# Seven half-size products for z over pairs of tiles

## The chip, the cores and the metric

The kernel runs on one core of a Trainium2 chip. The metric is the device time of one execution in microseconds (us), as the median of several runs. The engines of the core are TensorE (PE, matmuls, with its weight loads as PEld), VectorE (DVE), ScalarE (ACT), GpSimd (POOL) and SyncE (SP), which here only issues DMAs. They run their own queues and wait for each other by semaphores.

## The reference

```python
W = weights[condition]                         # x: (128, 64, 1024); 16 matrices of 64 x 64
y = einsum('bct,bcd->bdt', x, W)
z = einsum('bsd,od->bso', y, W_ffn) + b        # 1024 x 1024
u = einsum('bsd,edr->ebsr', y, A)              # 8 x 16 = 128 low-rank columns
m = einsum('ebsr,ero,e->bso', u, B, p_scores)
gamma = minimum(0.5 * norm(z) / (norm(m) + 1e-6), 1.0)    # norms over the last axis
out = x + z + gamma * m
```

Seen as a matrix, x has 128 x 64 = 8192 rows of 1024; all is float32.

## The kernel before

Two batches of 64 rows make a tile of 128 rows by 1024 columns; there are 64 tiles. The program has a body of four tiles, run once as an opening, in a loop, and once as a closing. All order is written out by hand, one function per engine, and all hand-offs are semaphores with counted waits.

For a tile, PE first mixes (`mix`, L416): for each of 8 chunks of 128 columns, the x chunk is the stationary operand and the block-diagonal 128 x 128 `mixer` of the two batches' matrices the moving one. So y comes out transposed, in two halves of 512 (half h of the 1024 summed columns) in PSUM `mix_ps`. These float32 matmuls appear as two instructions each, 8 a half. ACT casts y to `y_hi` in the fp32r type (L245), and DVE subtracts to get `y_lo` (L333). Every later product is the sum of three passes, hi x hi, hi x lo and lo x hi. W, A and B are held as hi and lo too; they are split once at the start by ACT and DVE (L241, L327).

`down` (L424) computes u for two tiles at once (256 moving columns, 8 chunks x 3 passes), `linear` (L443) half of z's columns for one tile (8 chunks x 3 passes of 512 moving columns, L439), `up` (L449) m for one tile (6 matmuls of 512 columns). DVE adds the bias to z out of PSUM (L368), ACT squares z and m with a row sum (L289, L313), POOL takes the roots as powers of 0.5 (L227, L232) and adds half of the residual x (L224), DVE the other half (L396), forms gamma and adds gamma times m (L408). SP loads x four tiles ahead into four slots, as soon as both residual halves of a tile are done, and stores the result.

PE's order for one tile in the loop: `down` (each second tile), `mix` of the tile two ahead, half 0; `linear` half 0; `up`; `mix` half 1; `linear` half 1. The mixer blocks are copied by ACT out of `cond_all`, which holds all 16 matrices (L248 to L255).

At the start, W arrives in eight chunks of 128 rows by 1024 (L174), tile 0's products follow the chunks, and tile 1's mix stands after the fifth chunk (L478).

Of the kernel before, what the change touches and what calls it, by code (L numbers as in the profile page):

```python
# [5 lines left out]
def conditioned_clamped_low_rank_linear_kernel(  # L6
# [43 lines left out]
    assert (C * PER, XR, H, D % P, TILES % BODY) == (P, P, 512, 0, 0) and STEPS >= 3

    x_tiles = x.rearrange("(n q) c t -> n (q c) t", q=PER)
    out_tiles = out.rearrange("(n q) c t -> n (q c) t", q=PER)

    ctx = ExitStack()
    with ctx:  # L59
# [21 lines left out]
        cond_ids = sb("cond_ids", [1, B], i32)
        p_col = sb("p_col", [P, 1], fp32)
        idle = sb("idle", [P, H], bf16)

        x_in = sb("x_in", [P, BODY, D], fp32)

        y_hi = sb("y_hi", [P, 2, KC, 2 * P], fp32r)
        y_lo = sb("y_lo", [P, 2, KC, 2 * P], fp32r)
# [9 lines left out]
        z_sum = sb("z_sum", [P, 2], fp32)
        half = sb("half", [P, 1], fp32)
        m_sq = sb("m_sq", [P, 2], fp32)  # L100
        norm_z = sb("norm_z", [P, 2], fp32)
        norm_m = sb("norm_m", [P, 2], fp32)
        twice_m = sb("twice_m", [P, 2], fp32)
        half_over_m = sb("half_over_m", [P, 2], fp32)
        gamma = sb("gamma", [P, 2], fp32)

        z_b = rows[:, 0:2, :]
        result = rows[:, 2:4, :]
        w_in = [rows[:, k, :] if k < 4 else w_late[:, k - 4, :] for k in range(KC)]
# [58 lines left out]
        def _(sp):

            sp.dma_start(cond_ids[:, :], condition.rearrange("(o n) -> o n", o=1)).then_inc(ids_loaded, 16)  # L170
            for q in range(PER):
                sp.dma_start(cond_all[q * C:(q + 1) * C, :, :], cond_w).then_inc(cond_loaded, 16)  # L172
            sp.dma_start(x_in[:, 0, :], x_tiles[0]).then_inc(x_loaded[0], 16)
            for k in range(KC):  # L174
                sp.dma_start(w_in[k], w[k * P:(k + 1) * P, :]).then_inc(w_loaded[k], 16)
                if k == MIX_1_AFTER:
                    sp.dma_start(x_in[:, 1, :], x_tiles[1]).then_inc(x_loaded[1], 16)
            sp.dma_start(x_in[:, 2, :], x_tiles[2]).then_inc(x_loaded[2], 16)
            sp.dma_start(a_in[:, :, :], a.rearrange("(k p) e r -> p k (e r)", p=P)).then_inc(a_loaded, 16)
            sp.dma_start(p_col[:, :], p_scores.rearrange("(e o) -> e o", o=1).unsqueeze(1)  # L180
                         .to_broadcast([X, R, 1])).then_inc(p_loaded, 16)
            sp.dma_start(bm_in[:, :], bm.rearrange("e r o -> (e r) o")).then_inc(bm_loaded, 16)
            sp.dma_start(bias[:, :], b.rearrange("(o n) -> o n", o=1).to_broadcast([P, D])).then_inc(bias_loaded, 16)
            for t in range(3, BODY):
                sp.dma_start(x_in[:, t, :], x_tiles[t]).then_inc(x_loaded[t], 16)

            def step(i, first, last):
                for j in range(BODY):
                    t = i * BODY + j
                    if not last:  # L190

                        sp.wait_ge(residual_0_ready, t + 1)
                        sp.wait_ge(residual_1_ready, t + 1)
                        sp.dma_start(x_in[:, j, :], x_tiles[t + BODY]).then_inc(x_loaded[j], 16)
                    if not (last and j == BODY - 1):
                        sp.wait_ge(out_ready, t + 1)
                        sp.dma_start(out_tiles[t], result[:, j % 2, :]).then_inc(out_stored[j % 2], 16)
                    else:

                        for h in range(2):  # L200
                            sp.wait_ge(out_ready, t + h + 1)
                            sp.dma_start(out_tiles[t][:, h * H:(h + 1) * H],
                                         result[:, j % 2, h * H:(h + 1) * H]).then_inc(out_stored[j % 2], 16)

            steps(sp, step)
            sp.wait_ge(out_stored[0], 16 * (TILES // 2))
            sp.wait_ge(out_stored[1], 16 * (TILES // 2 + 1))

        @block.gpsimd
        def _(pool):  # L210
            nc.gpsimd.memset(idle[:, :], 0.0).then_inc(idle_set, 1)
            nc.gpsimd.memset(half[:, :], 0.5).then_inc(half_set, 1)
            nc.gpsimd.memset(mixer[:, :, :], 0.0).then_inc(mixer_zeroed, 1)

            pool.wait_ge(half_set, 1)

            def step(i, first, last):
                for j in range(BODY):
                    t = i * BODY + j
                    one = slice(j % 2, j % 2 + 1)  # L220
                    if not first or j >= 2:
                        pool.wait_ge(out_stored[j % 2], 16 * (2 * i + j // 2))
                    pool.wait_ge(z_b_ready, 2 * t + 1)
                    nc.gpsimd.tensor_tensor(result[:, j % 2, 0:H], z_b[:, j % 2, 0:H], x_in[:, j, 0:H],  # L224
                                            ALU.add).then_inc(residual_0_ready, 1)
                    pool.wait_ge(m_squared, t + 1)
                    nc.gpsimd.tensor_tensor(norm_m[:, one], m_sq[:, one], half[:, :], ALU.pow).then_inc(norm_m_ready, 1)  # L227
                    pool.wait_ge(z_squared, 2 * t + 2)
                    nc.gpsimd.tensor_tensor(z_sum[:, one], z_sq[:, j % 2, 0:1], z_sq[:, j % 2, 1:2],  # L229
                                            ALU.add).then_inc(z_sum_ready, 1)  # L230
                    pool.wait_ge(z_sum_ready, t + 1)
                    nc.gpsimd.tensor_tensor(norm_z[:, one], z_sum[:, one], half[:, :], ALU.pow).then_inc(norm_z_ready, 1)  # L232
# [324 lines left out]
```

## Time and profile before

| | |
|---|---|
| median of 3 runs | 1031.13 us (1031.08 to 1031.2) |
| profiled execution | span 1029.6 us; no time of its own beside the span is given |
| busy: PE, DVE, ACT, POOL | 1017.3, 351.2, 289.2, 165.2 us |
| moved by DMA | 73.58 MB, mean 71 GB/s |
| instructions | 15207 |

The page's busy shares are of the span; PE's matmuls are pipelined, so that the start of one to the start of the next is shorter than the duration given for one. The spacing of matmuls is best read from the chain of waits, where a run of 24 has one duration.

### The profile page before, as it was taken

The page shows a single profiled execution, that of the slowest core. Times are in us where ns is not written, and L with a number is a line of the kernel's source. Part 1 is how long each engine was busy: PE and PEld are TensorE (multiplying, and loading weights), DVE is VectorE, ACT ScalarE, POOL GpSimd, SP SyncE. Part 2 cuts the span into 40 slices and gives each one's busy share as a digit, 9 for nine tenths or more (in the row PEclk, how much of TensorE's full clock was granted, in tenths as well). Part 3 has the DMA queues.
Part 4 walks back from the last instruction along what each step waited for, and adds up shares of the span by engine and source line. Part 5 has one row for each costly group of instructions (what it writes and reads, how often), then busy time and mean ns, then how long its engine had stood idle before and what let it go on. Part 6 is the DMA issues. An engine that isn't in the chain of part 4 may idle for free.

```text
span 1029.6 us, 15207 instructions
## 1 busy us (share of the span) xinstructions
PE 1017.3 (99%) x5260; PEld 856.4 (83%) x5260; DVE 351.2 (34%) x620; ACT 289.2 (28%) x685; POOL 165.2 (16%) x263
## 2 busy tenths in 40 slices
PE   7999999999999999999999999999999999999997
PEld 5888888888888888888888888888888888888885
DVE  4433233233333332332333333323323333233332
ACT  5322223223223322232232232222322322222211
POOL 0211111111111111111111111111111111111112
PEclk9999999999999999999999999999999999999999
DMA  8112122121221211211212212112112122121111
GB/s 324 52 74 79 44 81 75 48 81 41 81 81 41 81 66 57 81 61 61 81 41 81 81 41 81 61 62 81 57 65 81 41 81 81 41 81 49 74 42 41
DMA packets 21367, 73.58 MB, mean 71 GB/s; under 512 B 2409, under 2 KB 3434, under 8 KB 21354
## 3 DMA queue, kind: packets, MB, share of 16 engines
q1 hardware_dynamic: 21354, 73.41, 19.6%
q8 instruction: 8, 0.13, 0.1%
q14 instruction: 5, 0.04, 0.0%
HBM read 39.85 MB, written 33.55 MB: 71 GB/s over the span
## 4 chain that ended last, share of the span: by engine, by line
PE 98%; DMA 1%; DVE 0%; ACT 0%; SPq 0%; issue 0%; DVEq 0%; POOLq 0%; POOL 0%; ACTq 0%
PE z_ps L439 70%; PE mix_ps L419 11%; PE m_ps L456 9%; PE u_ps L430 9%; DMA x_in<-in_x_dram 1%; DVE w_lo L327 0%; SPq L172 0%; ACT w_hi L241 0%; DVE rows L408 0%; DVE rows L368 0%; DVEq L59 0%; ACT squares L289 0%; POOLq L59 0%; ACT y_hi L245 0%; SPq L170 0%
## 5 line engine op out<-in xcount | busy, mean ns | idle before, releaser
L439 PE MATMUL z_ps<-w_hi,y_hi 128*128 128x512 f32 x1024 | 415.9, 406 | 2.2 <-DVE w_lo L327 2.2
L439 PE MATMUL z_ps<-w_hi,y_lo 128*128 128x512 f32 x1024 | 405.8, 396 | 0.0
L439 PE MATMUL z_ps<-w_lo,y_hi 128*128 128x512 f32 x1024 | 405.4, 396 | 0.0
L289 ACT ACTIVATE squares<-rows 128x512 bf16<-128x512 f32 x128 | 80.8, 631 | 628.2 <-DVE rows L368 536.8
L439 PEld LDWEIGHTS z_ps<-w_hi,y_lo 128*128 128x128 f32 x1024 | 192.7, 188 | 46.3
L439 PEld LDWEIGHTS z_ps<-w_hi,y_hi 128*128 128x128 f32 x1024 | 193.4, 189 | 43.0 <-ACT y_hi L245 2.4
L439 PEld LDWEIGHTS z_ps<-w_lo,y_hi 128*128 128x128 f32 x1024 | 193.4, 189 | 40.9
L368 DVE TENSOR_TENSOR rows<-z_ps,bias 128x512 f32<-128x512 f32 x128 | 88.6, 692 | 365.7 <-PE z_ps L439 365.7
L333 DVE TENSOR_TENSOR y_lo<-mix_ps,y_hi 128x512 fp32r<-128x512 f32 x128 | 88.2, 689 | 232.7 <-ACT y_hi L245 232.5
L224 POOL TENSOR_TENSOR rows<-rows,x_in 128x512 f32<-128x512 f32 x64 | 81.7, 1277 | 428.0 <-DVE rows L368 428.0
L419 PEld LDWEIGHTS mix_ps<-mixer,x_in 128*128 128x128 f32 x1024 | 131.3, 191 | 10.8 <-DMA x_in<-in_x_dram 2.3
L419 PE MATMUL mix_ps<-mixer,x_in 128*128 128x128 f32 x1024 | 134.6, 275 | 1.7 <-DMA x_in<-in_x_dram 1.7
L408 DVE SCALAR_TENSOR_TENSOR rows<-m_ps,gamma,rows 128x1024 f32<-128x1024 f32 (+1 forms) x65 | 82.3, 1268 | 2.2
L245 ACT CAST y_hi<-mix_ps 128x512 fp32r<-128x512 f32 x128 | 73.3, 572 | 18.3 <-PE mix_ps L419 18.3
L430 PE MATMUL u_ps<-y_hi,a_hi 128*128 128x256 f32 x256 | 71.8, 280 | 0.0
L430 PE MATMUL u_ps<-y_lo,a_hi 128*128 128x256 f32 x256 | 71.6, 280 | 0.0
L430 PE MATMUL u_ps<-y_hi,a_lo 128*128 128x256 f32 x256 | 71.4, 279 | 0.0
L313 ACT ACTIVATE squares<-m_ps 128x1024 bf16<-128x1024 f32 x64 | 65.5, 1023 | 2.3 <-PE m_ps L456 0.5
L229 POOL TENSOR_TENSOR z_sum<-z_sq 128x1 f32<-128x1 f32 x64 | 12.3, 193 | 315.4 <-ACT squares L289 315.4
L227 POOL TENSOR_TENSOR norm_m<-m_sq,half 128x1 f32<-128x1 f32 x64 | 35.1, 548 | 111.0 <-ACT squares L313 111.0
L430 PEld LDWEIGHTS u_ps<-y_lo,a_hi 128*128 128x128 f32 x256 | 48.2, 188 | 1.4
L430 PEld LDWEIGHTS u_ps<-y_hi,a_hi 128*128 128x128 f32 x256 | 48.1, 188 | 1.4
(38 smaller groups left out, 479.8 us busy)
## 6 DMA issues: line engine op xcount, KB each, us to landing
x_in<-in_x_dram SPq DMA_DIRECT2D x64, 512.0 KB, 3.3
out_dram<-rows SPq DMA_DIRECT2D x63, 512.0 KB, 2.7
rows<-in_L_ffn_W_dram SPq DMA_DIRECT2D x4, 512.0 KB, 7.4
w_late<-in_L_ffn_W_dram SPq DMA_DIRECT2D x4, 512.0 KB, 11.0
cond_all<-in_L_cond_weights_dram SPq DMA_DIRECT2D x2, 256.0 KB, 4.0
a_in<-in_L_ffn_A_dram SPq DMA_DIRECT2D x1, 512.0 KB, 14.3
bm_in<-in_L_ffn_B_dram SPq DMA_DIRECT2D x1, 512.0 KB, 8.9
bias<-in_L_ffn_b_dram SPq DMA_DIRECT2D x1, 512.0 KB, 9.2
```

The costliest lines, as they stand in the source:

```text
L224: nc.gpsimd.tensor_tensor(result[:, j % 2, 0:H], z_b[:, j % 2, 0:H], x_in[:, j, 0:H], ALU.add).then_inc(residual_0_ready, 1)
L227: nc.gpsimd.tensor_tensor(norm_m[:, one], m_sq[:, one], half[:, :], ALU.pow).then_inc(norm_m_ready, 1)
L245: nc.scalar.copy(y_hi[:, j // 2 % 2, h * HC:(h + 1) * HC, j % 2 * P:(j % 2 + 1) * P], mix_ps[h][:, :].rearrange("p (k n) -> p k n", k=HC)) ...
L289: nc.scalar.activation(squares[:, cols], z_b[:, j % 2, cols], ACT.Square, accum_out=z_sq[:, j % 2, h:h + 1]).then_inc(z_squared, 1)
L313: nc.scalar.activation(squares[:, :], m_ps[:, :], ACT.Square, accum_out=m_sq[:, j % 2:j % 2 + 1]).then_inc(m_squared, 1)
L333: nc.vector.tensor_tensor(y_lo[part], mix_ps[h][:, :].rearrange("p (k n) -> p k n", k=HC), y_hi[part].bitcast(fp32), ALU.subtract).then_in ...
L368: nc.vector.tensor_tensor(z_b[:, j % 2, cols], z_ps[h][:, :], bias[:, cols], ALU.add).then_inc(z_b_ready, 1)
L408: nc.vector.scalar_tensor_tensor(out=result[:, j % 2, c], in0=m_ps[:, c], scalar=gamma[:, one], in1=result[:, j % 2, c], op0=ALU.mult, op1 ...
L419: mixed = nc.tensor.matmul(mix_ps[h][:, k * P:(k + 1) * P], x_in[:, j % BODY, (h * HC + k) * P:(h * HC + k + 1) * P], mixer[:, j % 2, :], ...
L430: summed = nc.tensor.matmul(u_ps[:, 0:2 * P], left[:, k, :], right[:, g, k, :], start=(k == 0 and n == 0), stop=(k == KC - 1 and n == 2))
L439: summed = nc.tensor.matmul(z_ps[h][:, :], left[:, g, k, r], right[:, k, h * H:(h + 1) * H], start=(k == 0 and n == 0), stop=(k == KC - 1 ...
L456: summed = nc.tensor.matmul(m_ps[:, c], left[:, r], right[:, c], start=(n == 0), stop=(n == 2))
```

## The change

Two tiles are taken together as a pair, and y of the pair is seen as a 2 x 2 matrix of blocks: rows by tile (r = 0, 1), columns by half h of the 1024 summed columns. Call them y00, y01, y10, y11. The transposed W is cut in four blocks of 512 x 512 in the same way: W11, W12, W21, W22 (first index the summed half, second the output half). Then

```
S3 = y00 - y10    S2 = y11 - S3    S1 = S2 + y00    S4 = y01 - S2
T1 = W12 - W11    T2 = W22 - T1    T3 = W22 - W12   T4 = W21 - T2
P1 = y00 W11   P2 = y01 W21   P3 = S4 W22   P4 = y11 T4   P5 = S1 T1   P6 = S2 T2   P7 = S3 T3
U2 = P1 + P6   U3 = U2 + P7
z tile 0: left P1 + P2, right U2 + P5 + P3      z tile 1: left U3 + P4, right U3 + P5
```

Each P is 4 chunks x 3 passes of 512 moving columns. P2 accumulates in PSUM on P1 (bank `b_ps`), P3 on P5 (`c_ps`); the sums U2, U3 and the halves of z are made by DVE in SBUF. The S blocks are made from PSUM and from float32 copies of tile 0's y (`s14`, by ACT): S3 and S2 by DVE, S1 and S4 by POOL. Each S is split in hi and lo by ACT and DVE as y is. T1 and T3 are made once by POOL, T2 and T4 by DVE; the seven W operands are held in hi and lo. The raw W blocks are loaded into places that later hold the lo (or hi) parts of other operands, so their loads and splits have a fixed order. W arrives in 16 pieces of 128 x 512.

x of a tile stays in its slot until the residual is added, as before; tile 1's residual is now one POOL operation of 1024 columns, tile 0's two of 512. y_hi and y_lo have one buffer, z of tile 1 one buffer, z of tile 0 two. The mixer is loaded by SP straight from DRAM, two DMAs of 64 x 64 for a tile at an index read by SP, and no longer copied by ACT.

The core of the diff; the new functions are shown by what they emit:

```diff
 # SP, in the loop, pair p
+    sp.wait_ge(residual1_ready, p)
+    sp.dma_start(x_in[:, 2 * (1 - j) + 1, :], x_tiles[2 * p + 3])
+    sp.wait_ge(mix_done, halves(2 * p + 1, 1));  load_mixer(2 * p + 3, 1)
+    sp.wait_ge(out1_ready, p)
+    sp.dma_start(out_tiles[2 * p - 1], z1[:, :])
+    sp.wait_ge(residual0_ready, 2 * p)
+    sp.dma_start(x_in[:, 2 * (1 - j), :], x_tiles[2 * p + 2])
+    load_mixer(2 * p + 2, 0)
+    sp.wait_ge(out0_ready, p)
+    sp.dma_start(out_tiles[2 * p - 2], z0[:, 1 - j, :])
 # POOL, at the start, after s1 and s4 of pair 0
+    bias[2] = bias[0] - bias[1]
+    for k in range(HC):  T1[k] = raw12[k] - raw11[k]
+    for k in range(HC):  T3[k] = raw22[k] - raw12[k]
 # POOL, in the loop
+    norm_z1(p - 1); residual1(p - 1); norm_m(p - 1, 1); make_s1(p)
+    norm_z0(p - 1); residual0(p - 1, h=1); make_s4(p); residual0(p, h=0); norm_m(p - 1, 0)
 # ACT, at the start
+    for h in range(2):  split_y(0, 0, h); copy_y(0, h)
+    split_w(W11); split_y(1, 1, 0); split_y(1, 1, 1); split_w(W21); a_hi
+    split_s(0, S2); split_s(0, S3); split_w(T2); split_w(T1); split_s(0, S1); split_u(0)
+    split_w(T3); split_w(W22); split_s(0, S4); split_w(T4); b_hi
 # ACT, in the loop
+    split_s(p, S2); square_z12(p - 1); split_s(p, S3); split_s(p, S1); split_s(p, S4)
+    square_z11(p); square_m0(p - 1); split_u(p)
+    for h in range(2):  split_y(2 * p + 2, 0, h); copy_y(p + 1, h)
+    for h in range(2):  split_y(2 * p + 3, 1, h)
+    square_z1(p); square_m1(p)
 # DVE, at the start
+    split_y(0, 0, 0); split_y(0, 0, 1); split_w(W11)
+    split_y(0, 1, 0); make_s3(0); split_y(0, 1, 1); make_s2(0)
+    split_w(W21, [0]); bias_p1(0); split_w(W21, [1, 2, 3]); a_lo; split_s(0, S2); split_s(0, S3)
+    make_z11(0)
+    for k in range(HC):  T2[k] = raw22[k] - T1[k];  T4[k] = raw21[k] - T2[k]
+    split_w(T2); split_w(T1); split_s(0, S1); make_u2(0); split_u(0)
+    split_w(T3); split_w(W22); split_s(0, S4); scale_b
+    make_u3(0); u3 + bias[2]; make_z22(0); split_w(T4); b_lo
+    split_y(1, 0, 0); split_y(1, 0, 1); z21; split_y(1, 1, 0); make_s3(1); split_y(1, 1, 1); make_s2(1)
 # DVE, in the loop
+    make_z12(p - 1); split_s(p, S2); make_gamma(p - 1, 1); add_m1(p - 1)
+    bias_p1(p); split_s(p, S3); split_s(p, S1); split_s(p, S4); make_z11(p)
+    dve.wait_ge(out1_stored, 16 * p);  z1[:, lo] = a_ps + bias[2]      # P4
+    make_gamma(p - 1, 0); add_m0(p - 1); split_u(p); make_u2(p)
+    split_y(p + 1, 0, 0); split_y(p + 1, 0, 1)
+    make_u3(p); z21: z1[:, lo] += z1[:, up_]; make_z22(p)
+    split_y(p + 1, 1, 0); make_s3(p + 1); split_y(p + 1, 1, 1); make_s2(p + 1)
 # DVE, after the last pair
+    make_gamma(1); add_m1; make_z12; make_gamma(0); add_m0
 # PE, pair 0
+    mix(tile 0); P1; mix(tile 1); P2; down; P6; P5; P7; mix(tile 2); P3; P4; mix(tile 3); up(1)
 # PE, in the loop
+    y_ready(2 * p, 0);      wait(u3_ready, p);             P1 -> b_ps
+    y_ready(2 * p + 1, 1);  down()
+    wait(p1_biased, p + 1);                                P2 -> b_ps
+    wait(out1_ready, p);                                   up(0, m_ps)      # of pair p - 1
+    wait(p4_biased, p - 1);                                P4 -> a_ps
+    s_ready(p, S2); wait(z11_ready, p + 1);                P6 -> b_ps
+    mix_next_0: wait x and mixer of tile 2 * p + 2, s3_made, s2_made
+    s_ready(p, S1); wait(z12_ready, p);                    P5 -> c_ps
+    s_ready(p, S3); wait(u2_ready, p + 1);                 P7 -> b_ps
+    mix_next_1: wait x and mixer of tile 2 * p + 3, y_lo_ready (both halves of tile 2 * p + 2)
+    u_ready(p);     wait(out0_ready, p);                   up(1, m_ps)
+    s_ready(p, S4); wait(z22_ready, p + 1);                P3 -> c_ps
+    # the last pair has no mix, and up(0) of its own after up(1)
```

`up(0, m_ps)` of a pair runs in the next pair's pass, after `down` of that one; `split_u` waits for it. `s_ready` is the wait for hi and lo of an S; `y_ready` the same for a half of a tile's y.

## Rows read from the trace of the kernel before

**Rows 1.** The page: busy us (share of the span) and count; granted clock in tenths.
```profile
PE 1017.3 (99%) x5260; PEld 856.4 (83%) x5260; DVE 351.2 (34%) x620; ACT 289.2 (28%) x685; POOL 165.2 (16%) x263
...
PEclk9999999999999999999999999999999999999999
```
**Rows 2.** The page: the chain that ended last, shares of the span by line.
```profile
PE z_ps L439 70%; PE mix_ps L419 11%; PE m_ps L456 9%; PE u_ps L430 9%; DMA x_in<-in_x_dram 1%; DVE w_lo L327 0%; SPq L172 0%; ACT w_hi L241 0%; DVE rows L408 0%; DVE rows L368 0%; DVEq L59 0%; ACT squares L289 0%; POOLq L59 0%; ACT y_hi L245 0%; SPq L170 0%
```
**Rows 3.** The chain over one pair, 521 to 553: start us, us, what.
```profile
521.38 2.80 PE u_ps L430 x24
524.18 0.89 PE mix_ps L419 x8
525.07 5.59 PE z_ps L439 x24
530.66 1.40 PE m_ps L456 x6
```
**Rows 4.** Windows: stretch, its us, busy us (count) per engine, clock, DMA.
```profile
450.00:481.55 31.55, 31.55 (x166) 26.68 (x165) 10.59 (x19) 8.70 (x21) 5.12 (x8) 1.00 0.18 66
```
**Rows 5.** Groups by form: line, engine, operation, shapes, count; busy us, mean ns; idle before.
```profile
L368 DVE TENSOR_TENSOR rows<-z_ps,bias 128x512 f32<-128x512 f32 x128 | 88.6, 692 | 365.7 <-PE z_ps L439 365.7
L333 DVE TENSOR_TENSOR y_lo<-mix_ps,y_hi 128x512 fp32r<-128x512 f32 x128 | 88.2, 689 | 232.7 <-ACT y_hi L245 232.5
L224 POOL TENSOR_TENSOR rows<-rows,x_in 128x512 f32<-128x512 f32 x64 | 81.7, 1277 | 428.0 <-DVE rows L368 428.0
L408 DVE SCALAR_TENSOR_TENSOR rows<-m_ps,gamma,rows 128x1024 f32<-128x1024 f32 x63 | 80.9, 1284 | 2.2
L289 ACT ACTIVATE squares<-rows 128x512 bf16<-128x512 f32 x128 | 80.8, 631 | 628.2 <-DVE rows L368 536.8 <-issue 91.4
L245 ACT CAST y_hi<-mix_ps 128x512 fp32r<-128x512 f32 x128 | 73.3, 572 | 18.3 <-PE mix_ps L419 18.3
L313 ACT ACTIVATE squares<-m_ps 128x1024 bf16<-128x1024 f32 x64 | 65.5, 1023 | 2.3 <-PE m_ps L456 0.5
...
L396 DVE TENSOR_TENSOR rows<-rows,x_in 128x512 f32<-128x512 f32 x64 | 44.3, 693 | 6.5
...
L227 POOL TENSOR_TENSOR norm_m<-m_sq,half 128x1 f32<-128x1 f32 x64 | 35.1, 548 | 111.0 <-ACT squares L313 111.0
...
L289 ACT ACTIVATION_READ_ACCUMULATOR squares<-rows 128x1 f32 x128 | 23.9, 187 | 0.0
```
**Rows 6.** Timeline from 506: start us, us, engine, line, operation, count, idle before.
```profile
506.83 1.05 PE L419 MATMUL mix_ps<-mixer,x_in 128*128 128x128 f32 x8
507.12 0.69 DVE L368 TENSOR_TENSOR rows<-z_ps,bias 128x512 f32<-128x512 f32 x1 [2.60 <-PE z_ps L439]
...
507.92 0.69 DVE L396 TENSOR_TENSOR rows<-rows,x_in 128x512 f32<-128x512 f32 x1
```
**Rows 7.** Windows at the start, columns as in rows 4.
```profile
12.30:16.20 3.90, 3.90 (x10) 3.08 (x11) 3.90 (x5) 3.33 (x6) 0.00 (x0) 0.56 1.04 414
```
**Rows 8.** The chain before PE's first product, and its last products.
```profile
12.14 0.14 issue
...
1017.08 5.61 PE z_ps L439 x24
```
**Rows 9.** Timeline of the start, of DVE, ACT and PE.
```profile
12.64 3.52 DVE L327 TENSOR_TENSOR w_lo<-rows,w_hi 128x1024 fp32r<-128x1024 f32 x3
...
16.95 1.05 ACT L241 CAST w_hi<-w_late 128x1024 fp32r<-128x1024 f32 x1 [1.29 <-DMA w_late<-in_L_ffn_W_dram]
...
12.27 0.47 PE L439 MATMUL z_ps<-w_hi,y_hi 128*128 128x512 f32 x1 [2.20 <-DVE w_lo L327]
...
13.27 0.63 PE L439 MATMUL z_ps<-w_hi,y_hi 128*128 128x512 f32 x1
13.70 0.63 PE L439 MATMUL z_ps<-w_lo,y_hi 128*128 128x512 f32 x1
```
**Rows 10.** DMA issues: names, engine, count, KB each, median us to landing.
```profile
x_in<-in_x_dram SPq DMA_DIRECT2D x64, 512.0 KB, 3.3
out_dram<-rows SPq DMA_DIRECT2D x63, 512.0 KB, 2.7
```

More of the change, by code:

```diff
@@ L81, in conditioned_clamped_low_rank_linear_kernel @@
[L81 to L88, printed above, removed]
+        x_in = sb("x_in", [P, 4, D], fp32)
+        y_hi = sb("y_hi", [P, KC, 2 * P], fp32r)
+        y_lo = sb("y_lo", [P, KC, 2 * P], fp32r)
+        s_hi = sb("s_hi", [P, 4, HC, P], fp32r)
+        s_lo = sb("s_lo", [P, 4, HC, P], fp32r)
@@ L98, in conditioned_clamped_low_rank_linear_kernel @@
[L98 to L109, printed above, removed]
@@ new lines, in conditioned_clamped_low_rank_linear_kernel, with stat @@
+        p_col = stats[:, 1:2]
+        table_out = stats[:, 2:3]
+        z11_sq, z12_sq = stats[:, 3:4], stats[:, 4:5]
+        def stat(n, r):
+            return stats[:, 6 + 2 * n + r:7 + 2 * n + r]
+        Z_SQ, M_SQ, NORM_Z, NORM_M, TWICE_M, HALF_OVER_M, GAMMA = range(7)
+        lo, up_ = slice(0, H), slice(H, D)
+        idle = squares[:, lo]
+        raw11 = w_hi_raw[:, T4, :, :]
+        raw21 = w_lo_raw[:, T4, :, :]
+        raw12 = w_lo_raw[:, T3, :, :]
+        raw22 = w_lo_raw[:, W22, :, :]
@@ new lines, in conditioned_clamped_low_rank_linear_kernel @@
+        raw = [raw11, raw21, raw12, raw22]
+        w_from = {W11: raw11, W21: raw21, W22: raw22, T3: raw12, T4: raw21,
+                  T1: w_lo_raw[:, T1, :, :], T2: w_lo_raw[:, T2, :, :]}
+        a_raw = a_lo_raw[:, :, :]
+        b_raw = b_lo_raw[:, :]
+        mix_ps = pb("mix_ps", [P, 2, H])
+        a_ps = pb("a_ps", [P, H])
+        b_ps = pb("b_ps", [P, H])
+        c_ps = pb("c_ps", [P, H])
+        m_ps = pb("m_ps", [P, D])
+        u_ps = pb("u_ps", [P, H])
+        m_last_ps = mix_ps[:, :, :].rearrange("p h n -> p (h n)")
@@ L213, in _, with norm_m @@
+            def norm_m(p, r):
+                pool.wait_ge(m_squared[r], p + 1)
+                nc.gpsimd.tensor_tensor(stat(NORM_M, r), stat(M_SQ, r), half, ALU.pow).then_inc(norm_m_ready[r], 1)
+            nc.gpsimd.memset(squares[:, :], 0.0).then_inc(idle_set, 1)
             nc.gpsimd.memset(mixer[:, :, :], 0.0).then_inc(mixer_zeroed, 1)
+            nc.gpsimd.memset(half, 0.5).then_inc(half_set, 1)
             pool.wait_ge(half_set, 1)
-            def step(i, first, last):
[L218 to L232, printed above, removed]
@@ new lines, in _ @@
+            act.wait_ge(half_set, 1)
+            nc.scalar.activation(table_out, half, ACT.Square).then_inc(table_loaded, 1)
+            for h in range(2):
+                split_y(0, 0, h)
+                copy_y(0, h, True)
+            split_w(W11)
+            for h in range(2):
+                split_y(1, 1, h)
+            split_w(W21)
+            act.wait_ge(a_loaded, 16)
+            nc.scalar.copy(a_hi[:, :, :], a_raw).then_inc(a_hi_ready, 1)
+            split_s(0, S2, True)
+            split_s(0, S3, True)
@@ L347, in _ @@
+            split_s(0, S2)
+            split_s(0, S3)
+            make_z11(0, 0)
+            for k in range(HC):
+                make_t24(k)
+            split_w(T2)
+            split_w(T1)
+            split_s(0, S1)
+            make_u2(0, 0)
+            split_u(0)
+            split_w(T3)
+            split_w(W22)
+            split_s(0, S4)
             dve.wait_ge(bm_loaded, 16)
             dve.wait_ge(p_loaded, 16)
-            nc.vector.tensor_scalar(bm_in[:, :], bm_in[:, :], p_col[:, 0:1], None, ALU.mult).then_inc(bm_scaled, 1)
@@ L412, in _ @@
-            steps(dve, step)
+            nc.vector.tensor_scalar(b_raw, b_raw, p_col, None, ALU.mult).then_inc(bm_scaled, 1)
+            make_u3(0, 0)
+            dve.wait_ge(u3_ready, 1)
+            dve.wait_ge(bias_difference_ready, 1)
+            nc.vector.tensor_tensor(z1[:, lo], z1[:, up_], bias[:, 2, :], ALU.add).then_inc(u3_biased, 1)
+            dve.wait_ge(u3_biased, 1)
+            make_z22(0)
+            split_w(T4)
+            dve.wait_ge(b_hi_ready, 1)
+            nc.vector.tensor_tensor(b_lo[:, :], b_raw, b_hi[:, :].bitcast(fp32), ALU.subtract).then_inc(b_lo_ready, 1)
@@ L427, in down, with u_ready @@
+            def u_ready(p):
+                pe.wait_ge(u_hi_ready, p + 1)
+                pe.wait_ge(u_lo_ready, p + 1)
+            def down():
                 for k in range(KC):
@@ L491, in _ @@
+            pe.wait_ge(p1_biased, 1)
+            product_y(b_ps, 0, 1, W21, False, True).then_inc(p_done[2], 1)
+            y_ready(1, 1)
             pe.wait_ge(a_hi_ready, 1)
             pe.wait_ge(a_lo_ready, 1)
-            down(0)
-            mix(2, 1)
+            down()
+            s_ready(0, S2)
+            pe.wait_ge(z11_ready, 1)
+            product_s(b_ps, S2, T2, True, True).then_inc(p_done[6], 1)
+            s_ready(0, S1)
+            product_s(c_ps, S1, T1, True, True).then_inc(p_done[5], 1)
@@ new lines, in step @@
+                    y_ready(2 * p, 0)
+                    pe.wait_ge(u3_ready, p)
+                    product_y(b_ps, 0, 0, W11).then_inc(p_done[1], 1)
+                    y_ready(2 * p + 1, 1)
+                    down()
+                    pe.wait_ge(p1_biased, p + 1)
+                    product_y(b_ps, 0, 1, W21, False).then_inc(p_done[2], 1)
+                    pe.wait_ge(out1_ready, p)
+                    up(0, m_ps)
+                    if first:
+                        pe.wait_ge(z21_ready, 1)
+                    else:
+                        pe.wait_ge(p4_biased, p - 1)
@@ L529, in _ @@
+                    product_s(b_ps, S3, T3).then_inc(p_done[7], 1)
+                    if not closing:
+                        mix_next_1(i, j, p)
+                    u_ready(p)
+                    pe.wait_ge(out0_ready, p)
+                    up(1, m_ps)
+                    if closing:
+                        up(0, m_last_ps)
+                    s_ready(p, S4)
+                    pe.wait_ge(z22_ready, p + 1)
+                    product_s(c_ps, S4, W22, False).then_inc(p_done[3], 1)
             steps(pe, step)
```

796 lines of the change are left out of this document (515 added, 281 removed).

## Prediction, made before the changed kernel was run

> **What bounds the kernel now.** I read the page's busy times first: TensorE (PE) is busy for 99% of the span at full granted clock, the next engine for 34% [rows 1]. The chain of waits says the same with more force: 98% of it is PE, of which z's products are 70% [rows 2]. Then the chain over one pair of tiles: it is unbroken PE work. 24 matmuls of 512 columns take 5.59 us, so one takes 0.233; six of the up product take 1.40, the same pitch; the 24 of the down product (256 columns) take 2.80, 0.117 each; one mix block (8) takes 0.89 [rows 3]. One pair is 96 z matmuls, 12 up, 24 down and four mix blocks: 22.37 + 2.80 + 2.81 + 3.57 = 31.55 us, and 31.55 us is what the window of one pair is, with DVE busy for 10.6 us of it and ACT for 8.7 [rows 4]. 32 pairs are 1009.6 us of the 1029.6 us span; some 20 us are start and tail. The page gives no time of its own for the profiled execution beyond its span; the span lies 1.5 us under the median of 1031.13, and I add 1.5 to the sum below.
>
> **The change, part by part.**
>
> *Products.* Seven products of 12 matmuls take the place of 96: 84, so 12 x 0.233 = 2.80 us less a pair. Down, up and mix stay as they are. New period if PE never waits: 31.55 - 2.80 = 28.75 us. A block of 12 costs no more per matmul than one of 24, since blocks of 6 already run at 0.233 [rows 3].
> The Trainium skill (TensorE: Matmul & The Clock Gate, Back-to-back issue gap) gives a warm matmul N/2.4 + 2.5 ns, 216 ns for 512 columns; by it the 12 would save 2.59 us a pair, 83 us over 32 pairs instead of 90. The row's 0.233 is used.
>
> *Can the other engines follow?* DVE now has, for each pair, 18 operations on 512 columns at 0.69 us, two 1024-wide adds at 1.28, and about 1.5 of small ones: 16.5 us of 28.75. ACT has ten casts or copies at 0.57, and three squares of 1024 and two of 512: 11.4 us. POOL has four 512-wide operations at 1.28 and one 1024-wide (put at twice that), with four powers at 0.55: 10.1 us [rows 5]. None is full, so only order counts. I walk the loop with time 0 at the start of P1 of a pair. PE then has P1 0-2.8, down -5.6, P2 -8.4, up(0) -9.8, P4 -12.6, P6 -15.4, mix of the next pair's tile 0 -17.2, P5 -20.0, P7 -22.8, mix of tile 1 -24.5, up(1) -25.9, P3 -28.7. Hand-offs: DVE starts 0.29 after the next PE block has begun, a DVE operation that waits for the one before starts 0.80 after its start [rows 6], and PE follows DVE by 0.14 [rows 8].
> - P3 waits for z22, behind make_u3, z21 and z22 on DVE. From the end of P7: 0.29 + 0.80 + 0.80 + 0.69 + 0.14 = 2.72 us. Its cover is mix and up, 1.79 + 1.40 = 3.19. Slack 0.47, or about 0.25 if the weight load, one matmul ahead, has to find the wait satisfied. This is the tightest place. Behind this wait stands the whole PE queue.
> - P2 waits for P1's bias add, which stands on DVE behind z12, one split, gamma and the 1.28 us add of tile 1. That add waits for POOL's residual of 1024 columns, which waits for ACT's square of z1. z22 lands at -3.3; square to -2.1; power to -1.5; residual to 1.0; power to 1.6; gamma and add to 3.5; bias add to 4.2; PE wants it at 5.6. Slack 1.3.
> - z11 (8.7-9.4) is wanted at 12.6, u2 (16.4) at 20.0, the sum that frees m_ps for up(1) (15.4) at 24.5, y_lo of the next tile (19.3) at 22.8. S1 to S4 are on hand by 7.7.
> - SP now issues the mixer's DMAs in line with x and the stores: x of tile 0 goes out at about 5 and lands 3.3 later [rows 10] against 15.4; tile 1 at about 1, against 22.8. If each 256-byte-row mixer load took as long as an x load, 3.3, it would still be ten us early. The moved mixer copies free 4 small ACT operations a pair, worth nothing. One store less in flight (z1 has one buffer): tile 1's store leaves at 3.6, P4's result wants the buffer at 12.8; slack 6.
> So the steady state costs 28.75 with bounds of 28.75 and about 29.5 (each hand-off of the P3 chain 0.2-0.3 later).
>
> *Start.* Here the change costs. Before, PE starts z at 12.27 and has no other stall worth naming, so the first pair ends near 43. After, the W parts must be made: DVE has 28 chunk splits of 0.60 pitch (three of double width take 3.52 [rows 9]), eight T2/T4 subtractions (1.40 a couple, since dependent), and pair 0's own 11 steps, in one queue, which PE follows. ids to mixer load to mix costs about what cond_all and x0 cost now: mix at 6.9, then y_hi, copy, y_lo: P1 from 11.6. After PE's idle of 2.2 us [rows 9] the mean granted clock of the next 3.9 us is 0.56, so most of it ran at the lower level, 1.2 GHz of 2.4 [rows 7], 0.43 us a matmul [rows 9]; I charge each idle of 2-4 us with the same, some 8 matmuls x 0.2 = 1.6. P1 to 16.0; mix of tile 1 to 17.7; W21's casts wait for tile 1's y_hi on ACT, and P1's bias add stands behind S3, S2 and one split on DVE: P2 21.5-26; down -28.8; z11 27.0; four T2/T4 couples to 32.6; P6 33.4-37.9; P5 -41.0; P7 -43.8; mix -45.5; DVE meanwhile T1, S1, T3, W22, S4, bm, u3, z22 to 47.6; P3 and P4 -54; mix, up(1) -57. Loading doesn't hold this: 512 KB arrive in 1.3 us [rows 9], 5.5 MB up to W22 in about 14 us from 5 on, before DVE wants them. If the bias, a 2 KB-row load or the slow p_col issue came 3 us later, one step moves by at most that.
> POOL adds one unknown. It makes s1, s4, the bias difference, four T1 and four T3 chunks between 20 and 34: eleven operations of 1.28 [rows 5] beside DVE operations whose both inputs lie in SBUF. In the trace of before no two such ones run side by side (the residual on POOL runs beside DVE operations with one PSUM input, and keeps its 1277 ns), so their cost together is bounded by 0 and by full turn-taking, 11 x 1.28 = 14 us, less 1.3 where DVE waits for P2 anyway: 13. I take 6: the nearest row speaks for 0, but half of these eleven fall between back-to-back DVE operations, and nothing shows that they go free. Pair 0 ends at 57 + 6 = 63 (bounds 54 and 71).
>
> *Tail.* The last P3 has no mix behind it. DVE then has gamma and add of tile 1, only then z12. From the end of the last P7: z22 at 2.6; ACT's square to 3.7; on POOL norm_z1 and norm_m1 (waiting for the next square) to 5.4, residual of 1024 columns to 8.0; add to 9.3; z12 to 10.1; square 11.0; two POOL norms 11.85; residual 13.2; add 14.5; store 3.2 more (2.7 [rows 10] and the last wait): 17.7. PE ends at 5.6 of these, so the tail is 12.1 us; before, it was 6.9 from 1022.69 to the end [rows 8].
>
> *Sum.* 63 + 31 x 28.75 (891.3) - 3.56 (the last pair's four mix blocks) + 1.40 (its additional up) + 12.1 = 964.2; + 1.5 = **965.7 us**, 6.3% less than 1031.1: 90 saved on products, 25 given back at the ends.
>
> **Rivals.**
> - *POOL and DVE take turns.* The eleven operations of the start hold DVE back in full. For it: W21_1 to S3 and the T2/T4 couples are queued without a gap, so each POOL operation finds DVE about to start. Against: the undisturbed 1277 ns. Gives +13 instead of +6: 972.7. In the loop it moves P1's bias add from 4.2 to 4.9, still under 5.6.
> The Trainium skill (SBUF — State Buffer, Who interferes with whom) states this: a DVE instruction with two SBUF inputs and a GpSimd one that reads SBUF lock each other out for the whole instruction. No run here shows it yet; by it the rival's 13 us hold.
> - *The P3 chain or the P2 chain is late in every pair.* Slack of 0.25-0.47 and 1.3 are sums of five to ten hand-offs. Each 0.1 us beyond costs 31 x 0.1 = 3.1 us. With three hand-offs 0.3 later, 0.5 us a pair: 965.7 + 15 = 981. Against: each term is a row of this trace.
> - *A better start*: the clock stays up after the idles (three times 1.6) and POOL costs nothing: 965.7 - 6 - 4.8 = 955.
> - *Slower than before: the clock falls in every pair.* At P3 PE would sit idle for 2.2 us or more, and the 3.5 us after it run at the 1.2 GHz level, 0.43 a matmul, as at 12.3-16.2 [rows 7, 9]: 2.2 + 1.6 = 3.8 a pair, 31 x 3.8 = 118 us: 1084. It decides from 65 / 31 = 2.1 us lost a pair, idle and slow matmuls together. The P3 chain would have to be 2.5 us longer than reckoned, so the rows speak against it.
>
> **How the numbers follow.** Forecast 0.45; turns in full 0.25; P3 or P2 late 0.17; better start 0.10; clock lost 0.03. Without the last, what is left lies between 950 (better start with a P1 1-2 us earlier and period unchanged, tail 2 shorter) and 984 (late chain of 0.5 us with a part of POOL's 7 more). Range 952 to 984. What a measurement can tell from no change is about 0.2%, 2 us; nothing of weight lies near 1031: faster 0.96, same 0.01, slower 0.03.
>
> **What would show it.** Period of 28.75 in the loop's windows, 166 - 12 = 154 matmul rows a pair (some rows group several), PE busy about 100% of it: the product step. Idle of PE before P3 (c_ps, first of S4 x W22) names the P3 chain; before the second product into b_ps, the P2 chain. PE's end of pair 0 at 57, 63 or 70 tells the POOL cases apart, and POOL's T1/T3 subtractions of 1.28 or longer with them. The tail from the last matmul: 12. Wrong would be the forecast if the loop's period isn't 28.7-28.9, or if a wait of PE on x or mixer loads comes up.

## The result, and the profile after

The changed kernel takes 952.99 us (median of 4, 952.67 to 954.46) against 1031.16 us for the kernel before: ratio 0.9245, 95% interval 0.9232 to 0.9258. Forecast was 965.7, range 952 to 984. The direction, the saving on products and the tail came as reckoned. The period of a pair and the start did not, and 12.7 us more came than was forecast. The profiled execution was the slowest of the four, 954.46 us with a span of 952.6.

The page first: busy times, and the granted clock in 40 slices.

```profile
PE 918.7 (96%) x4876; PEld 789.8 (83%) x4876; DVE 583.6 (61%) x903; ACT 357.7 (38%) x704; POOL 346.1 (36%) x336
...
PEclk8699999999999999999999999999999999999998
```

5260 - 4876 = 384 matmuls less, which is 32 x 12. PE is still the bound, and DVE is busy for 583.6 us instead of 351.2 [rows 1]. PE's idle time lies in the first three slices and in the last one. The windows' view of one period in the loop shows PE without a gap (columns as in [rows 4]):

```profile
478.75:507.50 28.75, 28.75 (x160) 24.97 (x158) 17.14 (x27) 11.11 (x23) 10.29 (x10) 1.00 0.23 82
```

A window of the forecast's width looks full whatever the period is; it holds 160 matmul rows here, where the forecast had 154. The period has to be read from equal blocks in the timeline. Here is PE's mix block of the next pair's tile 0 in two pairs, and between them the up product and the first row of P4 (start, us, what):

```profile
477.51 1.95 PE L739 MATMUL mix_ps<-mixer,x_in 128*128 128x128 f32 x16
...
498.97 0.62 PE L796 MATMUL m_ps<-b_hi,u_hi 128*128 128x512 f32 x2
499.42 0.62 PE L796 MATMUL m_ps<-b_lo,u_hi 128*128 128x512 f32 x2
499.88 0.61 PE L796 MATMUL m_ps<-b_hi,u_lo 128*128 128x512 f32 x2
500.33 0.39 PE L752 MATMUL a_ps<-w_hi,y_hi 128*128 128x512 f32 x1
...
505.77 1.95 PE L739 MATMUL mix_ps<-mixer,x_in 128*128 128x128 f32 x16
```

The period is 505.77 - 477.51 = 28.26 us, not 28.75. P4 and P6, 24 matmuls, fill the 5.44 us from 500.33 to 505.77, so one takes 0.2267, against 0.233 in [rows 3]. The same product on tensors of the same shape has become faster. No clock changed: it is 1.00 in both windows.

The start, in the timelines of PE, DVE and POOL (what ended an idle time in brackets):

```profile
11.32 0.47 PE L752 MATMUL b_ps<-w_hi,y_hi 128*128 128x512 f32 x1 [2.73 <-ACT w_hi L395]
...
15.74 1.95 PE L739 MATMUL mix_ps<-mixer,x_in 128*128 128x128 f32 x16
...
21.04 4.53 DVE L535 TENSOR_TENSOR w_lo<-w_lo_raw,w_hi 128x512 fp32r<-128x512 f32 x3
25.49 2.29 DVE L654 TENSOR_TENSOR a_lo<-a_lo_raw,a_hi 128x1024 fp32r<-128x1024 f32 x1
27.71 3.43 DVE L575 TENSOR_TENSOR s_lo<-s,s_hi 128x512 fp32r<-128x512 f32 x2
...
24.98 7.29 POOL L350 TENSOR_TENSOR w_lo_raw<-w_lo_raw,w_hi_raw 128x512 f32<-128x512 f32 x4
32.24 6.72 POOL L355 TENSOR_TENSOR w_lo_raw<-w_lo_raw 128x512 f32<-128x512 f32 x4
...
34.43 1.74 DVE L542 TENSOR_TENSOR w_lo_raw<-w_lo_raw 128x512 f32<-128x512 f32 x1
36.20 1.64 DVE L546 TENSOR_TENSOR w_lo_raw<-w_lo_raw 128x512 f32<-128x512 f32 x1
...
40.15 0.68 DVE L542 TENSOR_TENSOR w_lo_raw<-w_lo_raw 128x512 f32<-128x512 f32 x1
40.87 0.69 DVE L546 TENSOR_TENSOR w_lo_raw<-w_lo_raw 128x512 f32<-128x512 f32 x1
...
42.31 0.77 PE L752 MATMUL b_ps<-w_hi,s_hi 128*128 128x512 f32 x1 [9.37 <-DVE w_lo L535]
...
65.08 0.39 PE L752 MATMUL b_ps<-w_hi,y_hi 128*128 128x512 f32 x1
...
72.17 0.50 PE L752 MATMUL b_ps<-w_hi,y_hi 128*128 128x512 f32 x1 [1.35 <-DVE z L640]
```

POOL makes T1 and T3 from 24.98 to 38.96 (32.24 + 6.72), at 1.68 to 1.82 us an operation. From 32.9 on DVE's T2 and T4 operations take 1.64 to 1.74 us beside them, and 0.68 to 0.69 after them. PE sits idle for 9.4 us before P6. P1 takes 4.42 us for its 12 matmuls (11.32 to 15.74) at a mean granted clock of 0.61. Pair 0 ends at 65.08 (forecast 63), and pair 1 has one wait of 1.35 before P2.

The groups of the whole span name who is slowed (mean ns after the busy us):

```profile
L575 DVE TENSOR_TENSOR s_lo<-s,s_hi 128x512 fp32r<-128x512 f32 x128 | 142.1, 1129 | 4.9 <-ACT s_hi L413 0.6
L317 POOL TENSOR_TENSOR z<-z,x_in 128x512 f32<-128x512 f32 x64 | 82.7, 1293 | 130.4 <-ACT squares L428 130.4
L305 POOL TENSOR_TENSOR s<-s 128x512 f32<-128x512 f32 x32 | 55.8, 1745 | 0.0
L350 POOL TENSOR_TENSOR w_lo_raw<-w_lo_raw,w_hi_raw 128x512 f32<-128x512 f32 x4 | 7.3, 1853 | 0.0
L620 DVE TENSOR_TENSOR z<-b_ps,z 128x512 f32<-128x512 f32 x32 | 22.1, 692 | 111.6 <-PE b_ps L752 111.6
```

DVE with one PSUM input keeps its 692 ns; the S split, with two SBUF inputs, takes 1129 ns on average; POOL's S4, which runs beside it, 1745 instead of 1277 [rows 5].

The chain of waits covers the tail (start, us, what):

```profile
940.02 0.55 POOL stats L336
940.57 2.31 POOL z L311
...
943.35 1.28 DVE z L607
944.63 0.61 DVE z L630
...
945.27 0.63 ACT squares L435
...
946.94 1.24 POOL z L317
...
948.28 1.28 DVE z L600
```

These are the tail's steps in the order that the prediction gave: norm_m1, residual, add, z12, square, residual, add. PE's last product starts at 937.83 (the last up pair at 937.37 plus two spacings) and takes 12 x 0.2267, so it ends at 940.55; the tail is 952.6 - 940.55 = 12.1 us, as forecast.

### The profile page after: what moved, and what is told of

It reads as the page before. It is cut to its first block and busy times, and to the rows that moved or that the text cites. A ratio compares the mean times of both kernels' runs of the same rounds, so it can differ in the third digit from the quotient of the medians.

```text
span 952.6 us, 15191 instructions
## 1 busy us (share of the span) xinstructions
PE 918.7 (96%) x4876; PEld 789.8 (83%) x4876; DVE 583.6 (61%) x903; ACT 357.7 (38%) x704; POOL 346.1 (36%) x336
## 5 line engine op out<-in xcount | busy, mean ns | idle before, releaser
L575 DVE TENSOR_TENSOR s_lo<-s,s_hi 128x512 fp32r<-128x512 f32 x128 | 142.1, 1129 | 4.9 <-ACT s_hi L413 0.6
L752 PE MATMUL b_ps<-w_hi,y_hi 128*128 128x512 f32 x256 | 102.1, 399 | 7.9 <-DVE z L640 4.8
L752 PE MATMUL b_ps<-w_hi,s_hi 128*128 128x512 f32 x256 | 100.5, 392 | 9.4 <-DVE w_lo L535 9.4
L752 PE MATMUL c_ps<-w_hi,s_hi 128*128 128x512 f32 x256 | 102.4, 400 | 1.9 <-issue 1.8
L752 PE MATMUL b_ps<-w_lo,y_hi 128*128 128x512 f32 x256 | 101.3, 396 | 0.0
L752 PE MATMUL b_ps<-w_hi,y_lo 128*128 128x512 f32 x256 | 101.1, 395 | 0.0
L752 PE MATMUL b_ps<-w_lo,s_hi 128*128 128x512 f32 x256 | 100.3, 392 | 0.0
L752 PE MATMUL b_ps<-w_hi,s_lo 128*128 128x512 f32 x256 | 100.1, 391 | 0.0
L752 PE MATMUL c_ps<-w_lo,s_hi 128*128 128x512 f32 x256 | 99.8, 390 | 0.0
L752 PE MATMUL c_ps<-w_hi,s_lo 128*128 128x512 f32 x256 | 99.8, 390 | 0.0
```

The source lines that it names most:

```text
L575: nc.vector.tensor_tensor(s_lo[:, n, :, :], s_raw(n), s_hi[:, n, :, :].bitcast(fp32), ALU.subtract).then_inc(s_lo_ready, 1)
L752: summed = nc.tensor.matmul(bank[:, :], left[:, k, :], right[:, n, k, :], start=(start and k == 0 and i == 0), stop=(k == HC - 1 and i == ...
```

## Experiments

The first four tell the start's contention and the matmul spacing apart.

**POOL's T subtractions as memsets.**
```diff
-                nc.gpsimd.tensor_tensor(w_from[T1][:, k, :], raw12[:, k, :], raw11[:, k, :], ALU.subtract
-                                        ).then_inc(t1_made, 1)
+                nc.gpsimd.memset(w_from[T1][:, k, :], 0.0).then_inc(t1_made, 1)
 # and T3 in the same way
```


> The changed kernel, with POOL's eight T1 and T3 subtractions of the start replaced by memsets of the same places behind the same waits (T1 and T3 are zero, so z is not the reference's). DVE's own work is the same. Theory (POOL and DVE operations that both read SBUF, DVE with two SBUF inputs, take turns): DVE's T2/T4 couples fall from 1.7 us an operation to 0.7, the a_lo and S splits before them too; P6 starts near 35 instead of 42.3, and the kernel takes 945 to 947 us. Rival (the long DVE times are its own, from dependences or from loading): P6 stays at 42, 953 us.

946.63 us (ratio 0.9181, 0.9165 to 0.9196). The timeline of DVE and PE:
```profile
27.56 0.69 DVE L544 TENSOR_TENSOR w_lo_raw<-w_lo_raw 128x512 f32<-128x512 f32 x1
28.17 0.69 DVE L540 TENSOR_TENSOR w_lo_raw<-w_lo_raw 128x512 f32<-128x512 f32 x1
...
32.98 0.77 PE L750 MATMUL b_ps<-w_hi,s_hi 128*128 128x512 f32 x1 [4.61 <-DVE w_lo L533]
```
P6 starts at 33.0 instead of 42.3. 1.6 of that is P1, which in this execution ran at full clock, 2.86 us instead of 4.42 for the same 12 matmuls:
```profile
11.28 0.47 PE L750 MATMUL b_ps<-w_hi,y_hi 128*128 128x512 f32 x1 [2.74 <-DVE w_lo L533]
...
14.14 1.95 PE L737 MATMUL mix_ps<-mixer,x_in 128*128 128x128 f32 x16
...
19.45 4.53 DVE L533 TENSOR_TENSOR w_lo<-w_lo_raw,w_hi 128x512 fp32r<-128x512 f32 x3
```
The rest, 7.7 us, is what the eight subtractions cost. The rival (the long DVE times are DVE's own) falls. POOL's first three operations (S1, S4, the bias difference) are still in this kernel, and DVE's three W21 splits beside them take 4.53 us as before; what those three cost was not tried.

**The kernel before with 32 bytes of padding.**
```diff
         idle = sb("idle", [P, H], bf16)
+        pad = sb("pad", [P, 8], fp32)
```


> The kernel before with 32 bytes of padding in SBUF ahead of x_in, so that x_in, y_hi, y_lo, u_hi and u_lo start at multiples of 64 bytes; no instruction changes. Theory (the spacing of matmuls, 0.2331 us before and 0.2267 after, depends on where the stationary operand starts): z and up products go to 0.2267, down perhaps from 0.117 to 0.120; a pair falls by 108 x 0.0064 - 24 x 0.003 = 0.6 us, 32 pairs by 20 us: 1011 us. Rival (the spacing comes from the PSUM banks, the products' order or the layout of W): nothing moves, 1031 us.

1032.14 us, ratio 1.001 (1.0 to 1.0019), where the theory had 1011: no gain. The theory in this form, a multiple of 64, fails.

**The changed kernel with 32 bytes of padding.**
```diff
+        pad = sb("pad", [P, 8], fp32)
         x_in = sb("x_in", [P, 4, D], fp32)
```


> The changed kernel with 32 bytes of padding ahead of x_in, so that x_in, y, S and u start 32 bytes off a multiple of 64. Theory (start of the stationary operand): spacing goes from 0.2267 to 0.2333, the period from 28.26 to about 28.8, 31 periods and pair 0: 953 + 17 to 19 = 971 us. Rival (banks, order, layout of W): 953 us.

968.77 us (0.9399, 0.9383 to 0.9415), 15.8 us slower than the changed kernel for 32 bytes of unused memory. The mix blocks show the period:
```profile
483.24 1.95 PE L740 MATMUL mix_ps<-mixer,x_in 128*128 128x128 f32 x16
...
505.00 0.63 PE L797 MATMUL m_ps<-b_hi,u_hi 128*128 128x512 f32 x2
505.47 0.63 PE L797 MATMUL m_ps<-b_lo,u_hi 128*128 128x512 f32 x2
505.94 0.63 PE L797 MATMUL m_ps<-b_hi,u_lo 128*128 128x512 f32 x2
512.00 1.95 PE L740 MATMUL mix_ps<-mixer,x_in 128*128 128x128 f32 x16
```
28.76 us, the forecast's 28.75 but for 0.01, with 0.233 a matmul again. So the places in SBUF matter here, and did not there.

**T1 and T3 made by DVE.**
```diff
+            for k in range(HC):          # on DVE, ahead of the T2/T4 couples; T3 ahead of split_w(T3)
+                nc.vector.tensor_tensor(w_from[T1][:, k, :], raw12[:, k, :], raw11[:, k, :], ALU.subtract
+                                        ).then_inc(t1_made, 1)
```


> The changed kernel with T1 and T3 made by DVE in its own queue instead of by POOL: eight subtractions of 512 columns more on the engine that PE follows in the start. Theory (taking turns): each costs DVE 0.6 us where it stretched DVE's operations by about 1.1 when POOL made it, so the start is 3 to 5 us shorter, 948 to 950 us, with DVE's T2/T4 operations at 0.7 us each. Rival (no contention): DVE's queue grows by 8 x 0.6 = 4.8 us, 958 us.

950.49 us (0.9217, 0.9202 to 0.9233). Eight operations more on the engine that PE waits for make the kernel 2.5 us faster, half a microsecond short of the range expected. The T2 and T4 operations take 0.68 to 0.69 us.

The next four look for the rule of the spacing, and test the slack and the tail.

**96 bytes of padding in the kernel before** (the pad of the second experiment with 24 elements).

> The kernel before with 96 bytes of padding ahead of x_in, so that x_in, y and u start at multiples of 128 bytes (32 bytes of padding, which put them 64 off, moved nothing: 1032.1 us). Theory (a stationary operand that starts at a multiple of 128 bytes has a spacing of 0.2267 us for 512 columns, every other tried start 0.2333): period 31.55 - 108 x 0.0066 + 24 x 0.003 = 30.91, 32 pairs by 20.5 us: 1010 to 1012 us. Rival (32 bytes off is a loss in the changed kernel for a reason of its own, such as where S or its z lie, and the kernel before stays as it is): 1031 us.

1030.8 us, ratio 0.9997 (0.9988 to 1.0006): no change. A start at a multiple of 128 isn't the rule. The chain shows a small trade (us for 24):
```profile
521.09 2.88 PE u_ps L431 x24
...
524.86 5.57 PE z_ps L440 x24
```
z's 24 take 5.57 to 5.59 instead of 5.59 to 5.60, down's rose from 2.80 to 2.88.

**One more DVE operation in the chain to P3.**
```diff
                     dve.wait_ge(z21_ready, p + 1)
+                    nc.vector.tensor_tensor(z1[:, lo], z1[:, lo], z1[:, lo], ALU.max).then_inc(extra_ready, 1)
+                    dve.wait_ge(extra_ready, p)
                     make_z22(p)
```


> The changed kernel with one more DVE operation of 512 columns (z1's left half, maximum with itself) between z21 and z22 in every pair from the second on, each waiting for the one before: 0.73 us more in the chain to P3. By the prediction's slack of 0.25 to 0.47 PE would then wait 0.26 to 0.48 us in each of 31 pairs: 961 to 968 us. By the trace after (z22 ends 0.75 us before P3 starts, 0.53 before its weight load) it would be 0 to 0.2 us a pair: 953 to 959 us. If the P3 chain had much more slack than either: 953 us.

961.32 us (0.9327, 0.9309 to 0.9344). In the timeline z22 ends at 490.37 + 0.69 = 491.06, and P3 follows 0.14 later:
```profile
490.37 0.69 DVE L636 TENSOR_TENSOR z<-c_ps,z 128x512 f32<-128x512 f32 x1
490.63 0.61 PE L799 MATMUL m_ps<-b_hi,u_lo 128*128 128x512 f32 x2
...
491.20 0.47 PE L755 MATMUL c_ps<-w_hi,s_hi 128*128 128x512 f32 x1
```
Its mix blocks stand 28.50 us apart, 0.24 more than 28.26. 0.73 was added, so 0.49 us of it were free, by which P3 is the next bound of the loop. The prediction had 0.47, or 0.25 with a deduction for the weight load. The two numbers agree in part by chance. In the changed kernel z22 ends 0.75 us before P3 starts (458.90 and 459.65); with 0.14 for the hand-off that is a slack of 0.61, as the chain is shorter than was reckoned. Once P3 is late, it costs more than its lateness: of the 0.24, half is the wait, and half lies in P3 itself, 2.84 us instead of 2.72; the weights of its first matmul are now loaded at 491.17, 0.03 us ahead of it instead of 0.22.

**Another order in the tail.** DVE makes z12 first, POOL tile 1's residual ahead of norm_m1 (POOL's part is left out of the diff).
```diff
+            make_z12(PAIRS - 1, 1)
             make_gamma(PAIRS - 1, 1)
             add_m1(PAIRS - 1)
-            make_z12(PAIRS - 1, 1)
```


> The changed kernel with another order after the last pair: DVE makes z12 before it waits for tile 1's gamma and sum; POOL makes tile 1's residual before the power for its norm of m. Theory (the tail is the chain that the prediction walked, POOL's residual, add, z12, square, norms, residual, add): z12 is made at PE's end + 0.3, the second residual follows POOL's norms at once, and the last add starts about 3 us earlier: 949.5 to 950.5 us. Rival (the tail is set by the last store or by m's square): 953 us.

950.32 us (0.9216, 0.9203 to 0.9229), 2.7 less. From the start of the last up pair to the end of the span the changed kernel takes 952.6 - 937.37 = 15.2 us, this one 951.1 - 939.01 = 12.1.

**The three together**, with the scaling of B behind z22.

> T1 and T3 on DVE (950.5 us alone), the tail's other order (about -3), and the scaling of B on DVE moved behind z22 of pair 0, out of P3's way (-0.7). If the three lie in different places and add up: 946 to 947.5 us, faster than both kernels. If DVE's queue as a whole sets the start, the move of the scaling gives nothing: 947.5 us.

948.33 us (0.9197, 0.9185 to 0.921), faster than both kernels. In the profiled executions P6 starts at 35.41 (35.74 with T1 and T3 on DVE alone), P3 at 51.97 (53.01), and pair 0 ends at 61.06 (61.72). So the move of the scaling brought P3 forward by its 0.7, but only half of that reached the end of the pair: DVE's queue up to the next split of y is no shorter, and PE waits 0.3 us for that split before its last mix block. The median is 0.8 us above the upper end of what was expected; runs of this kernel spread by more (946.97 to 948.76).

**480 bytes of padding in the kernel before** (120 elements). W, A and B start at 128 modulo 512 in both kernels; y, S and u do so in the changed kernel, and with this padding in the kernel before too.

> The kernel before with 480 bytes of padding ahead of x_in: y, u and x_in now lie at the same place modulo 512 bytes as W, A and B do (128), which is also so in the changed kernel. Theory (what counts is that stationary and moving operand start at the same place modulo 256 or 512): spacing 0.2267, 1010 to 1012 us. Rival (the SBUF places matter only as multiples of 32, and the other half of the changed kernel's gain comes from its banks, order or W layout): at most 1030 us, as with 96 bytes.

1014.19 us (0.9828, 0.9812 to 0.9844): 17 us off the kernel before with no instruction changed. The chain (us for 24, and for 6):
```profile
522.26 1.36 PE m_ps L457 x6
523.62 0.89 PE mix_ps L420 x8
524.51 5.46 PE z_ps L440 x24
```

**128 bytes of padding in the changed kernel** (32 elements).

> The changed kernel with 128 bytes of padding ahead of x_in: y, S, u and x_in move from 128 to 256 modulo 512, W stays at 128. Theory (same place modulo 256 or 512 counts): spacing 0.2317 to 0.2333, 967 to 971 us as with 32 bytes. Rival (multiples of 128 are all alike in this kernel): 953 us.

969.88 us (0.9404, 0.9387 to 0.9421). Multiples of 128 are not alike.

**Matmuls that keep PE busy in pair 0**, on top of the combined version; their results are thrown away.
```diff
+            def keep_busy(count):
+                for _ in range(count):
+                    nc.tensor.matmul(a_ps[:, :], w_hi[:, W11, 0, 0:P], w_hi[:, W11, 0, :], start=True, stop=True)
 # keep_busy(13) before P2, (22) before P6, (6) before P7, (10) before P3
```


> The combined version with 51 additional matmuls in pair 0 whose results are thrown away (into P4's bank before P4), put where PE waits for DVE: 13 before P2, 22 before P6, 6 before P7, 10 before P3. Theory (the 1.2 GHz stretches of the start come from PE's idle stretches, and DVE's queue sets most of the start): P2, P6 and P3 run at 0.227 a matmul, which is worth 1 to 3 us: 945.5 to 947.5 us against 948.3. If the matmuls at the lower clock did not set the end at all: 948.3. If the added ones stand in the way: 950 or more.

947.03 us (0.9177, 0.9162 to 0.9193), the fastest median of all; its interval overlaps the combined version's, so the 1.3 us between them are not shown. The clock is (windows from 20 to 60 us, this kernel, then the combined one):
```profile
20.00:60.00 40.00, 33.59 (x167) 26.42 (x166) 39.13 (x57) 18.85 (x35) 6.58 (x4) 1.00 0.23 84
```
```profile
20.00:60.00 40.00, 28.74 (x130) 22.14 (x129) 38.27 (x56) 18.87 (x35) 5.23 (x4) 0.83 0.23 84
```
Full clock instead of 0.83, and little gained: DVE is busy for 38 to 39 of these 40 us and sets this stretch. The two executions differ before it, too: P1 takes 4.41 us in this one and 2.82 in the combined one, so P2 starts 1.3 us later, and pair 0 still ends only 0.5 later (61.55, 61.06).

**224 bytes of padding in the kernel before** (56 elements): y at 384 modulo 512, so 128 modulo 256 as W.

> The kernel before with 224 bytes of padding ahead of x_in: y, u and x_in lie at 384 modulo 512 against W's 128, so the same modulo 256 and different modulo 512. If the same place modulo 256 is enough: spacing 0.2267 for 512 columns, 1012 to 1015 us as with 480 bytes. If it must be the same modulo 512: about 1031 us, as with 32 and 96 bytes.

1013.66 us (0.983, 0.9813 to 0.9846). The same place modulo 256 is enough.

## Why the prediction was right, and where it was off

The time lies in the range, near its lower end of 952, but not for the reason that end had. It stood for a better start, and the start came 2.1 us later than forecast; the faster matmuls made up for it. By the prediction's own sign, a period of 28.7 to 28.9 us, the forecast was wrong: it is 28.26. That the range held is in this part luck.

- *Products, 12 less a pair*: right. 384 matmuls went, and PE has no gap in the stretches of the loop that were looked at.
- *Spacing of 0.233*: the term that was mis-sized. It was read from [rows 3] and carried over as a price of the shape. It is 0.2267 where y, S and u start at the same place modulo 256 bytes as W and B. That they do is luck: in the kernel before, the one column p_col, which takes 32 bytes, is placed ahead of x_in and y and shifts them, and in the changed kernel it lies behind them, in `stats`. 31 periods x (28.75 - 28.26) = 15.2 us less than forecast. With 32 bytes of padding the period was 28.76. The Trainium skill (TensorE: Matmul & The Clock Gate, Back-to-back issue gap) gives 216 ns for an isolated matmul of 512 columns, and about 131 ns in a sustained stream; the streams of these runs took 226.7 to 233 ns.
- *P3's chain as the tightest place*: right; 0.73 more in it cost 0.24 a pair. Its terms partly cancel (see the experiment). P2's chain had no wait in the loop either, but one of 1.35 us in pair 1, which the prediction did not walk.
- *Start*: mis-sized. The allowance of 6 us for POOL and DVE was too small, and pair 0 ended at 65.1, not 63. The eight subtractions alone cost 7.7 us at P6, and 7.5 at the end of pair 0 (65.1 to 57.6 with the memsets; P1 at full clock gained 1.6 there, P3 at the lower clock lost 1.6). Between the medians it is 6.4 us. So the measured price lies between the 6 that was taken and the 13 of the rival with full turns. The three operations before the eight are not in it. The rule of the Trainium skill (SBUF — State Buffer, Who interferes with whom) holds in the rows: with both at work a DVE and a POOL operation together took 1.64 to 1.82 us, nearly the 0.6 + 1.28 of taking turns, and memsets, which read nothing, left DVE at 0.67 to 0.69.
- *The walk without contention*: P6 at 33.4 was forecast, and 33.0 came with the memsets, but in part by cancelling: P2 started at 19.6, not 21.5, as P1 ran at full clock, and the three W21 splits took 4.53 us, where eight splits later on take 4.90.
- *The charge for the clock* (1.6 us for each idle): the size was right in PE's own rows; what it is worth depends on the place. P1 at the lower clock, 4.42 us against 2.86, moves P2 by 1.6, since DVE's next work waits for the mix behind P1. P3 at the lower clock, 4.42 us with the memsets against 2.82, moves the end of pair 0, since from P3 on PE sets it. At P6, DVE's queue sets the next step, and it costs next to nothing. Which blocks are slow differs between executions of the same code: the kernel with another tail is the same up to there, and its P3 took 4.41.
- *Tail of 12.1*: right, and so was each step of its chain, within 0.3 us.
- *512 KB in 1.3 us*: read from a wait of ACT [rows 9], which is not the time of an arrival; the 414 GB/s of [rows 7] give the same 1.3. No load held the start.
- The span's sum: 964.2 forecast, -15.2 (spacing), +2.1 (start), +1.35 (pair 1's wait), +0.1 (not traced): 952.6. The median, 952.99, is 12.7 below 965.7 where the span is 11.6 below 964.2, since the profiled execution was 1.5 us slower than the median, and its time 1.9 above its span instead of 1.5.

## What to carry to other kernels

When the change adds or resizes tensors, a matmul spacing read from the old trace is a price of the old addresses too; try a pad before the large operands. Read a period from two equal blocks, not from a window of the expected width. In a start that one engine's queue sets, giving work to POOL can cost more than doing it there, as it did here with both reading SBUF. Walk the first steady iteration and the last one as closely as the loop.

## What was not expected of the hardware

For fp32r products with 128 stationary and 512 moving columns, the spacing depends on where the stationary operands (y, S, u) start in SBUF, modulo 256 bytes. The table counts from the start of the moving operands (W, B). These lie at 128 modulo 256 in every run, so it is not shown whether the distance between the two counts or the place of y, S and u by itself; a run with W and B moved would tell. The starts are the byte addresses in a partition at which the built program places its tensors: w_hi at 16512 in both, y_hi at 125600 before (distance 109088, 32 modulo 256) and 171136 after (154624, 0 modulo 256). Medians in us, padding in brackets:

| distance modulo 256 | kernel before | changed kernel |
|---|---|---|
| 0 | 1013.7, 1014.2 us (224, 480 bytes) | 953.0 (none) |
| 32 | 1031.1 (none) | 968.8 (32 bytes) |
| 64 | 1032.1 (32 bytes) | |
| 128 | 1030.8 (96 bytes) | 969.9 (128 bytes) |

With a pad x_in, y, S, u and all that is placed behind them moved together; which of them counts was not tried alone, but up, which uses only u and B, and z changed alike. Down, with 256 moving columns (there y moves, and A is stationary), went the other way: 2.80 us for 24 at distance 32, 2.88 at 128 (above) and 2.87 in the changed kernel at 0. Why is open.
